# Who normalises the last batch's attention output: GpSimd behind its own queue, or VectorE behind two other queues

## The reference, cut to what matters

```python
x = x + 0.5 * _L0_ffn_ref(_layernorm(x), w_gate, w_up, w_down)
x = x + _L0_attn_ref(_layernorm(x), Wq, bq, Wk, bk, Wv, bv, Wo, bo)
x = x + 0.5 * _L0_ffn_ref(_layernorm(x), w_gate, w_up, w_down)
x = x + 0.5 * _L1_ffn_ref(_layernorm(x), w1, b1, w2, b2)
x = x + _L1_attn_ref(_layernorm(x), Wq, Wk, Wv, Wo, bo)      # causal, with rotary positions
x = x + 0.5 * _L1_ffn_ref(_layernorm(x), w1, b1, w2, b2)
```

```python
probs = jax.nn.softmax(scores, axis=-1)
intervened = probs.at[:, :, :, 0].set(0.0)
intervened = intervened / jnp.clip(intervened.sum(-1, keepdims=True), 1e-09, None)
combined = probs + 0.5 * (intervened - probs)
attn_out = einsum('bhqk,bhkd->bhqd', combined, V)     # then @ Wo.T + bo
```

## Time and profile before

| | |
|---|---|
| median of 3 runs | 2335.18 us (2333.16 to 2338.78) |
| profiled execution | 2329.27 us |
| its span, first to last instruction | 2326.7 us |
| mean granted TensorE clock | 0.953 |
| PE busy | 2085.1 us (90%) |
| DVE busy | 1621.4 us (70%) |
| ACT busy | 1334.7 us (57%) |
| POOL busy | 519.9 us (22%) |
| `out_stage` of layer 0 | about 982 to 1045 us |
| `out_stage` of layer 1 | about 2084 to 2124 us |

### The profile page before, as it was taken

The page is one execution under the profiler, slowest core; times in us unless marked ns, Lnnn a source line. Parts: engine busy times, 40 slices in busy tenths (PEclk is TensorE's granted clock), DMA queues, the critical chain, the costliest instruction groups (busy, mean ns, idle before and its releaser), DMA issues. The chain is left out here.

```text
span 2326.7 us, 45876 instructions
## 1 busy us (share of the span) xinstructions
PE 2085.1 (90%) x17861; PEld 1304.2 (56%) x17861; DVE 1621.4 (70%) x2087; ACT 1334.7 (57%) x2564; POOL 519.9 (22%) x567
## 2 busy tenths in 40 slices
PE   4999689999999999859969998839999999987998
PEld 3887533333333333348858887615555555546888
DVE  7776499999999999246774447947777777716433
ACT  3443258888888888604434553306667677652444
POOL 2000321211321411440021113762221212112110
PEclk9999879999999999979979999958999999999999
DMA  4004732433534442110030001693444545310000
GB/s 137 1 0 172 236 58 43 72 75 58 107 63 86 79 81 51 51 45 1 0 115 1 0 0 64 195 183 66 80 92 80 102 94 101 67 53 19 28 18 27
DMA packets 124765, 162.76 MB, mean 70 GB/s; under 512 B 55321, under 2 KB 78617, under 8 KB 124569
## 3 DMA queue, kind: packets, MB, share of 16 engines
q1 hardware_dynamic: 107352, 120.72, 24.3%
q0 software_dynamic: 17216, 39.37, 6.3%
HBM read 95.04 MB, written 63.70 MB: 68 GB/s over the span
## 5 line engine op out<-in xcount | busy, mean ns | idle before, releaser
L1460 DVE TENSOR_REDUCE att_maxes<-att_s_max 128x2 f32<-128x1024 f32 (+2 forms) x832 | 973.9, 1183 | 189.0 <-PE att_s_max L1281 88.5
L1439 ACT ACTIVATE att_probs<-att_s_exp 128x512 f32<-128x512 f32 (+3 forms) x1792 | 888.0, 552 | 242.5 <-PE att_s_exp L1338 117.4
L1362 PE MATMUL att_o_ps<-att_probs,att_v_st 128*32 128x256 f32 (+1 forms) x6912 | 526.3, 376 | 14.9 <-ACT att_o_sb L1418 14.2
L1338 PE MATMUL att_s_exp<-att_q_st,att_k_st 64*128 64x512 f32 (+3 forms) x1792 | 459.5, 474 | 4.4 <-ACT att_probs L1439 3.9
L1298 PE MATMUL att_s_max<-att_k_st,att_q_st 62*128 62x512 f32 (+3 forms) x1792 | 395.6, 418 | 69.0 <-POOL att_k_st L1508 33.3
L1338 PEld LDWEIGHTS att_s_exp<-att_q_st,att_k_st 64*128 64x128 f32 x1792 | 189.7, 184 | 343.1 <-ACT att_probs L1439 295.0
L1362 PEld LDWEIGHTS att_o_ps<-att_probs,att_v_st 128*32 128x32 f32 x6912 | 138.0, 108 | 256.8 <-issue 140.5
L1298 PEld LDWEIGHTS att_s_max<-att_k_st,att_q_st 62*128 62x128 f32 x1792 | 189.2, 194 | 92.4 <-issue 56.6
L1533 POOL TENSOR_TENSOR att_m_parts<-att_m_turned,att_zeros 32x128 fp32r<-32x128 f32 x64 | 28.9, 451 | 530.1 <-ACT att_m_turned L1405 390.3
L587 DVE TENSOR_TENSOR ffn1b_h_lo<-ffn1b_h,ffn1b_h_hi 128x512 fp32r<-128x512 f32 x64 | 45.0, 704 | 111.0 <-PE ffn1b_acc L135 99.2
L1546 POOL DMA_DIRECT2D attention_rows<-att_o_sb x64 | 37.5, 586 | 358.6 <-ACT att_o_sb L1418 358.6
(11 more groups left out here) (296 smaller groups left out, 3997.7 us busy)
## 6 DMA issues: line engine op xcount, KB each, us to landing
att_q_st<-q_parts SPq DMA_DIRECT2D x384, 64.0 KB, 5.2
att_k_st<-k_parts SPq DMA_DIRECT2D x192, 128.0 KB, 4.9
attention_rows<-att_o_sb POOLq DMA_DIRECT2D x64, 256.0 KB, 3.8
output_wide<-attention_weights POOLq DMA_DIRECT2D x48, 256.0 KB, 5.2
q_parts<-qkv_parts SPq DMA_DIRECT2D x16, 512.0 KB, 3.8
k_parts<-qkv_parts SPq DMA_DIRECT2D x16, 512.0 KB, 2.7
v_rows<-qkv_vt SPq DMA_DIRECT2D x16, 512.0 KB, 4.5
att_v_raw<-v_rows SPq DMA_DIRECT2D x32, 256.0 KB, 6.3
```

The lines of the kernel that those rows point to most:

```text
L1338: mm = pe.matmul(s_exp[:, plan.bank[place], q0:512], k_st[rows, it.set, pr, kt * P:(kt + 1) * P], q_st[rows, it.set, qc, pr, q0:512], star ...
L1362: mm = pe.matmul(o_ps[j * VW:(j + 1) * VW, cols], v_st[:, it.par, kt, j, :], probs[:, step % 2, j, cols], start=kt == 0 and part == 0, sto ...
L1439: act.activation(probs[:, step % 2, j, q0:512], s_exp[:, plan.bank[place], q0:512], ACT.Exp, scale=1.0 if causal else 0.25).then_inc(s["ex ...
L1460: v.tensor_reduce(maxes[:, qc, :, pairs, qt - 4 * qc, kc], banks, AX.X, ALU.max).then_inc(s["max_done"], 1)
```

## The change

Five edits:

1. Batch 3 is no longer multiplied by POOL (`normalise_outputs`) but by DVE, in a new `normalise_last(half)` that DVE runs after its work on chunk 4 (half 0) and on chunk 5 (half 1).
2. Its spread DMAs are issued by SP (features 0 to 127) and by ACT (features 128 to 255), both halves at once, the second into a buffer of its own, `wide_last`. There are two semaphores, `last_in0` and `last_in1`.
3. Inside `out_stage`, `invert_totals` becomes DVE's first instruction, `invert_shares` follows the statistics of chunk 0, the `normalise` for the next stage goes from DVE to POOL behind `store_weights`, and the turn on PE and `part_lo` move from chunk 5 to chunk 6.
4. The attention block ends with `no_gpsimd_drain=True`: at its end the other engines don't wait until GpSimd has drained its DMA work.
5. PE's first chunk in `ffn_stage`, `qkv_stage` and `rope_stage` doesn't wait for the two counts.

```diff
+RSTD_STEPS = 5
@@ ffn_stage, PE
-                    if f == 0:
+                    if f == 0 and not first:
                         pe.wait_ge(s["hi_ready"], c * KD + KD)
                         pe.wait_ge(s["lo_ready"], c * KD + KD)
@@ qkv_stage, PE (rope_stage alike, with "if c:")
-                pe.wait_ge(s["hi_ready"], c * KD + KD)
-                pe.wait_ge(s["lo_ready"], c * KD + KD)
+                if not first:
+                    pe.wait_ge(s["hi_ready"], c * KD + KD)
+                    pe.wait_ge(s["lo_ready"], c * KD + KD)
@@ spread_weights
-def spread_weights(p, E, b, half):
+def spread_weights(p, E, b, half, wide, landed, of=range(KD)):
     n = E.o_sem
     p.wait_ge(n["weights_out"], 16 * (b + 1))
     for kind in range(E.kinds):
-        for k in range(KD):
+        for k in of:
             heads = E.w_dram[b, kind, k * H // KD:(k + 1) * H // KD, half * CHUNK:(half + 1) * CHUNK]
-            p.dma_start(E.wide[:, kind, k, :], heads...).then_inc(n["wide_in"], 16)
+            p.dma_start(wide[:, kind, k, :], heads...).then_inc(landed, 16)
@@ attention_stage
-        block = ctx.enter_context(nc.Block())
+        block = ctx.enter_context(nc.Block(no_gpsimd_drain=True))
@@ out_stage
+        wide_last = ctx.enter_context(nc.sbuf_tensor(f"{name}_wide_last", [P, E.kinds, KD, CHUNK], F32))
-        TURN_AT = 5
+        TURN_AT = 6
+        @block.sync
+        def _(sp):
+            spread_weights(sp, E, LAST, 0, E.wide, E.o_sem["last_in0"], (0,))
+            spread_weights(sp, E, LAST, 1, wide_last, E.o_sem["last_in1"], (0,))
@@ scalar
             norm_root(act, E, s["next_var"], s["next_std"], NEXT)
+            spread_weights(act, E, LAST, 0, E.wide, E.o_sem["last_in0"], (1,))
+            spread_weights(act, E, LAST, 1, wide_last, E.o_sem["last_in1"], (1,))
             part_hi(act, E, T, 0, 0, s)
@@ vector
+            def normalise_last(half):
+                n = E.o_sem
+                wide = (E.wide, wide_last)[half]
+                v.wait_ge(n["o_in"], 16 * KD * B)
+                v.wait_ge(n[f"last_in{half}"], 16 * KD * E.kinds)
+                at = slice(LAST * S + half * CHUNK, LAST * S + (half + 1) * CHUNK)
+                rest = E.o_t[:, :, at]
+                if E.kinds == 1:
+                    v.tensor_tensor(rest, rest, wide[:, 0, :, :], ALU.mult).then_inc(n["normal"], 1)
+                    return
+                v.tensor_tensor(rest, rest, wide[:, 0, :, :], ALU.mult).then_inc(s["scaled"], 1)
+                v.wait_ge(s["scaled"], half + 1)
+                for k in range(KD):
+                    ins = v.scalar_tensor_tensor(out=E.o_t[:, k, at], in0=wide[:, 1, k, :], scalar=E.v_first[:, LAST, k:k + 1],
+                                                 in1=E.o_t[:, k, at], op0=ALU.mult, op1=ALU.add)
+                ins.then_inc(n["normal"], 1)
+            invert_totals(v, E, LAST)
...
+                if c == 0 and E.kinds == 2:
+                    invert_shares(v, E, LAST)
                 if c == 0:
                     measured.then_inc(s["next_step"], 1)
...
                 if c == 1:
-                    invert_totals(v, E, LAST)
                     norm_rstd(v, E, s["next_step"], s["next_std"], NEXT, n)
-                if c == 2:
-                    if E.kinds == 2:
-                        invert_shares(v, E, LAST)
-                    normalise(v, E, 0, 0, s)
+                if c == 4:
+                    normalise_last(0)
+                if c == 5:
+                    normalise_last(1)
@@ gpsimd
             store_weights(p, E, LAST)
-            for half in range(2):
-                spread_weights(p, E, LAST, half)
-                normalise_outputs(p, E, LAST, half)
+            p.wait_ge(s["next_step"], 1 + NORM_STEPS + RSTD_STEPS)
+            normalise(p, E, 0, 0, s)
```

More of the change, by code:

```diff
@@ L815, in _ @@
                 par = c % 2
-                pe.wait_ge(s["hi_ready"], c * KD + KD)
-                pe.wait_ge(s["lo_ready"], c * KD + KD)
+                if c:
+                    pe.wait_ge(s["hi_ready"], c * KD + KD)
+                    pe.wait_ge(s["lo_ready"], c * KD + KD)
                 for kind, w in enumerate((E.wq, E.wk)):
@@ L1054, in alloc_outputs @@
     E.o_sem = semaphores(nc, E, name, "stored0", "stored1", "sums_in", "o_in", "total", "total_inv", "share", "share_inv", "step",
-                         "weights", "weights_out", "wide_in", "first_in", "product", "normal")
+                         "weights", "weights_out", "wide_in", "last_in0", "last_in1", "first_in", "product", "normal")
 def fetch_outputs(p, E, b, last):
@@ L1123, in spread_weights @@
     for kind in range(E.kinds):
-        for k in range(KD):
+        for k in of:
             heads = E.w_dram[b, kind, k * H // KD:(k + 1) * H // KD, half * CHUNK:(half + 1) * CHUNK]
-            p.dma_start(E.wide[:, kind, k, :], heads.unsqueeze(1).to_broadcast([H // KD, HD, CHUNK])).then_inc(n["wide_in"], 16)
+            p.dma_start(wide[:, kind, k, :], heads.unsqueeze(1).to_broadcast([H // KD, HD, CHUNK])).then_inc(landed, 16)
 def normalise_outputs(p, E, b, half):
@@ L1571, in body @@
                         normalise_outputs(p, E, b, 0)
-                        spread_weights(p, E, b, 1)
+                        spread_weights(p, E, b, 1, E.wide, E.o_sem["wide_in"])
                     store(it, 0)
@@ L1582, in body @@
                     elif it.hg == 2:
-                        spread_weights(p, E, b, 0)
+                        spread_weights(p, E, b, 0, E.wide, E.o_sem["wide_in"])
                     elif it.hg == 3:
@@ L1602, in out_stage @@
         T = ctx.enter_context(nc.psum_tensor(f"{name}_T", [P, KD, CHUNK], F32))
-        s = semaphores(nc, E, name, "turned", "hi_ready", "lo_ready", "out_done", "x_new", "xn_ready", "next_step", "next_var", "next_std")
+        wide_last = ctx.enter_context(nc.sbuf_tensor(f"{name}_wide_last", [P, E.kinds, KD, CHUNK], F32))
+        s = semaphores(nc, E, name, "scaled", "turned", "hi_ready", "lo_ready", "out_done", "x_new", "xn_ready", "next_step", "next_var", "next_std")
         block = ctx.enter_context(nc.Block())
         LAST = B - 1
-        TURN_AT = 5
+        TURN_AT = 6
         @block.tensor
```

## The result

| | before | after |
|---|---|---|
| median, taken on the same chip | 2334.17 us (4 runs) | 2297.43 us (4 runs, 2295.88 to 2299.93) |
| profiled execution | 2329.27 us | 2296.3 us |
| mean granted TensorE clock | 0.953 | 0.958 |
| PE busy | 2085.1 us | 2084.8 us |
| DVE busy | 1621.4 us | 1627.3 us |

A forecast was written before the change was run, and what follows sets the result against it. Stage ends bound it: each stage's last engine sets the next start, with holes after attention and in the out stages' tails. Gains 31.0 + 10.7 + 0.5 = 42.2 us give 2287.1 profiled; plus 5.9, 2293.0 us; range 2285 to 2305.

The forecast's parts named there:

- The drain: Out stages: without it PE starts 0.3 us after the store's issue; worth 5.6 us in layer 0, 5.2 in layer 1.
- the drain is not what fills the gap: Rival, both out stages: engines start as late as now, 5.6 + 5.2 us lost again, 2303.8 us; chance 0.08.
- DVE's chain: Layer 0's out stage: DVE's reordered work sums to 31.6 us, next stage at 1014.0 against 1045.01, minus 31.0 us.
- POOL disturbs DVE's new work: Rival, `normalise_last`: multiplications take 3.36 us, not 1.21, giving 2304.4; chance 0.13 together with half that cost or late spreads.
- The spreads: Layer 0's out stage: half 0 usable at 997.4, half 1 at 1002.4; slack 1.7 and 2.0 us.
- the rival of the late spreads: Out stages: spreads 2 to 5 us late, 2296 to 2299 us; chance 0.13 together with POOL disturbing DVE.
- PE's clock after a wait: Layer 0's out stage: PE was taken at full clock, 3.7 us a chunk, chunk 6 from 1001.8 to 1005.5.
- the stage end: Layer 1, after attention: store ends at 2079.1, PE starts at 2079.4, DVE at 2084.7 in place of 2089.92.
- The counts: First chunks of feed-forward and projection stages: not waiting for them gains 0.5 us in all, bounds 0 and 2.

The follow-up runs named there:

- a3: The changed kernel with the drain behind attention and the waits for the counts put back (edits 1 to 3 alone): 2308.39 us, ratio 0.9896.
- a1: The kernel before with edit 4 alone, no drain behind attention: 2323.16 us, ratio 0.996.
- b4: The changed kernel with SP and ACT issuing half 1's spreads only when half 0 has landed: 2301.04 us, ratio 0.9853.
- b1: The changed kernel with all of batch 3's spreads issued from POOL's queue, both buffers kept: 2292.38 us, ratio 0.9821.
- c3: The same code as b1 (all spreads from POOL's queue), run again beside c0: 2292.8 us, ratio 0.9829.
- a4: The changed kernel with the waits for the counts put back (edits 1 to 4): 2299.54 us, ratio 0.9868.
- b3: The changed kernel with half 0's spreads issued from POOL's queue, half 1's still from SP's and ACT's: 2300.72 us, ratio 0.986.
- c0: The changed kernel itself, run again beside the last experiments: 2297.0 us, ratio 0.9847.
- c1: The changed kernel with layer 0's `invert_totals` moved behind chunk 0's statistics and `invert_shares` behind `norm_variance`: 2299.67 us, ratio 0.9859.
- a2: The kernel before with edit 5 alone, no wait for the counts in first chunks: 2333.29 us, ratio 0.9997.
- c2: The diffs of c1 and b1 together on the changed kernel: `invert_totals` behind chunk 0, all spreads from POOL: 2293.18 us, ratio 0.9828.

## Why the prediction was right, and where it was off

Predicted were 2293.0 us in a range of 2285 to 2305; measured 2297.43. Part of that closeness is luck. The sum was made against the profiled execution and came to 2287.1; that measured 2296.3, 9.2 us more. The prediction then added 5.9 us, the distance of the old profiled execution from the median. The new one lies only 1.1 below its median. In spans, 42.2 us were predicted and 32.3 came: 9.9 us short. They divide into 3.9 in layer 0's out stretch, 2.5 in layer 1's, 1.85 and 1.2 in two feed-forward stages, and 0.5 for the counts.

**The drain: right.** The sum had 5.6 and 5.2 us for it, 10.8; a3 against the changed kernel gives 4.6 and 6.2, 10.8. That the sums are equal is luck: one layer is 1.0 below, the other 1.0 above. DVE's chunk 0 in layer 0 did move by 5.55 us (12.66 to 7.11); the stage end got 0.9 less, 0.7 of it because DVE waited longer for chunk 6, which took 6.32 us and not 5.41. The way through the total and the reciprocal, 982.1 less 975.2 or 6.9 us from the store's issue to DVE's chunk 0, measured 7.11. The rival "the drain is not what fills the gap" is out: a1 alone removes layer 0's gap and halves layer 1's. Alone the edit gave more in layer 0, 8.5 us in a1's trace: 6.9 by PE's start, since DVE has no reciprocal ahead of chunk 0 there, and 1.65 by the clock of chunk 0, which was half in six of the eleven traces without a drain.

**DVE's chain: right.** Chunks 0 to 4 took 16.7 us, and 17.0 were worked out; `normalise_last` took 1.23 and 1.42 us for 2.7 predicted; layer 1's single multiplication 1.21 for 1.3. The rival "POOL disturbs DVE's new work" did not come: POOL's `normalise` was over at 997.93, 5.5 us before DVE's first multiplication. Its 4.83 us lie between the bounds of 3.1 and 6.3, hidden.

**The spreads: the term that failed.** "Four spreads were usable 7.8 us after the first issue: half 0 at 997.4" was to leave a slack of 1.7 us. Measured are an issue at 991.75 (14.55 us after the store's, 14.4 predicted) and 11.7 us to use. Of the 3.9 us too much, b4 gives 2.4 to half 1 in flight beside it. The other 1.5 are there when half 0 moves alone on these queues. The assumption of the old rate for both halves together, five us apart, is what fell: the rate was that of POOL's queue (b1 and c3 have it, 7.9 and 8.1 us), and on two queues half 0 doesn't move ahead of half 1 undisturbed. (The 5 us are themselves short of the prediction's own 7.8 less 2.4, 5.4; nothing hangs on it.) DVE waited 2.46 and 0.19 us. This is the rival of the late spreads ("2 to 5 us late"), in layer 0 alone.

The Trainium skill, "DMA: Bandwidth & Descriptors", section "Issuing engines are not separate DMA queues", says that DMAs issued by several engines share the same 16 DMA engines, so that a second issuer saves only time to issue. For SP and ACT against SP alone the runs agree: two queues had half 0 ready later than one (11.7 and 10.0 us). For POOL's queue against these they don't: the same reads ran at about 200 GB/s in place of about 140, which that sentence doesn't foresee. The measurement decides.

**PE's clock after a wait: left out.** The prediction let chunk 6 run in 3.7 us. PE was idle for 4.59 us before it and the 16 matmuls then took 6.32 us, so DVE waited 0.91 and 0.41 us for chunks 6 and 7. In the changed kernel that is a second bill for the same late DMA: 1.3 us on top of 2.65. Not all of it is sure to go when the DMA is in time. In b1, with 2.21 us idle, chunk 6 still took 5.41, and DVE waited 0.29 and 0.41; in c3, the same code with the same 2.21, it took 3.72 and DVE did not wait. Of the kernels with the new tail, the six with 4.5 us or more of idle time before chunk 6 (the changed kernel, a3, a4, b3, c0, c1) all took 5.4 to 6.4.

**Layer 1: the stage end was mis-sized.** The prediction took 0.3 us between the end of the store's issue and PE's start, from a stage end without a fresh DMA. In layer 0 that was even too long; in layer 1 it measured 2.3 us (1.8 to 2.6 in all kernels without the drain), and PE's chunk 0 then ran at the low clock, 5.30 us. DVE's chunk 0 came 8.25 us after the store's issue (6.2 predicted), which is 2.05 of the 2.5 us. That the weights' store would be held up behind the loads of `o_t` was right (landed after 7.1 us, 1.9 before); spreads issued 13.8 us after the store's issue (11.5 predicted) were still in time.

**The counts: 0.5 predicted, none found** (a2, a4).

**Two stages outside.** The first feed-forward was 1.85 us longer. The view by windows (us; busy us and count for each engine; then granted clock, DMA share, GB/s) has the granted clock there. The changed kernel, with the start of the last stage beside it:

```profile
176.00:178.00 2.00, 2.00 (x10) 1.90 (x9) 0.88 (x2) 0.63 (x1) 0.00 (x0) 0.50 0.00 0
2090.30:2093.50 3.20, 3.20 (x8) 2.53 (x9) 3.05 (x9) 0.00 (x0) 3.20 (x5) 0.50 0.00 0
```

And the kernel before:

```profile
176.00:178.00 2.00, 2.00 (x12) 1.66 (x11) 0.69 (x1) 0.96 (x2) 0.00 (x0) 1.00 0.00 0
2124.00:2127.00 3.00, 2.87 (x12) 2.17 (x12) 2.86 (x5) 0.00 (x0) 3.00 (x5) 1.00 0.00 0
```

At 176 us both kernels have just had the same pause of PE of 2.36 us, and came out of it at 1.2 GHz in one and at 2.4 in the other. b3 has every edit of that stage too and took 155.32 us, and a1 has none of them and took 157.9, so this is not the change. Over all fourteen traces it follows the clock in the 2 us behind that pause: where it was 1.00 (before and b3) the stage took 155.1 and 155.3 us, where it was 0.50 to 0.86 it took 156.6 to 158.3. The last stage is different: it took 204.1 to 204.6 us in every kernel whose last out stretch is under 39 us, and 202.7 to 203.1 in the four others (before, a1, a2, a3). It begins at half clock in the changed kernel and at full clock before; in the four short ones the first 3 us have a granted clock of 0.71 to 1.00, in the ten long ones 0.50 to 0.64. That this accounts for the 1.2 us fits the rows but was not tried by itself.

**What stays open.** Why the queues of SP and ACT leave the 16 engines half idle on these reads while POOL's keeps them 87% busy: the traces show packets of 2 KB against 4 KB, but no experiment changed the reads' size or pattern. Why the end of layer 1's attention takes 2.3 us and layer 0's nothing. And what decides PE's clock behind a pause of 1.5 to 2.4 us.

## What to carry to other kernels

In this kernel a stage whose last work is a fresh DMA issued by POOL paid for its drain: look for a gap of 5 to 7 us behind the last store, with a queue and no DMA as its releaser, and count what the next stage's first instructions really need. A landing time holds for the queue it was measured on; when a transfer moves to other queues, price it by a row of those queues, and keep what is wanted first ahead in one queue. Where such a transfer is late, add the slow matmuls that can follow PE's pause. And before a change of 1 us in one stretch is put down to an edit, look whether PE's clock fell the same way in both traces.

## What the runs showed of the hardware that I had not expected

- The same reads (one row of DRAM to 16 partitions, 256 KB each) ran at about 140 GB/s with two hardware queues, the 16 engines 46% busy, in packets of 2 KB, and at about 200 GB/s from POOL's queue, the engines 87% busy, in packets of 4 KB. One hardware queue alone was no slower than two.
- Two halves in flight at once delayed the first by 2.4 us (b4), and by more when they came from queues of both kinds (b3: DVE waited 5.96 us).
- POOL's `normalise` took 4.83 us while DVE ran its adds from PSUM, 5.26 us in b1 and 6.01 in c2, where it overlapped `normalise_last`; DVE's two L1646 then took 1.59 us in place of 1.42, and the multiplication ahead of them its usual 1.21 to 1.23. The Trainium skill, "SBUF — State Buffer", section "SBUF: two separate sides", says that a DVE instruction with both inputs in SBUF and a POOL instruction shut each other out; the direction agrees, but here it cost DVE 0.17 us, a small part of what the rival had put on it.
- PE's clock after the same pause was half in one trace and full in another, for pauses of 1.46, 2.21 and 2.36 us, once between two traces of the same code (b1 and c3). Where a stage that no edit touches differs by 1 to 3 us, look for this first: in the first feed-forward stage it was this.
